# A local attention slot in a new order: GpSimd makes the low parts of the weights and the first squares

## What is computed

```python
for i in range(6):
    x = attn_layer(shift_tokens(x), Wqkv[i], q_scale[i], k_scale[i], Wo[i]) + x
    x = ffn_layer(shift_tokens(x), ln_g[i], ln_b[i], W1[i], b1[i], W2[i], b2[i]) + x

def attn_layer(x, Wqkv, qs, ksc, Wo):        # 16 heads of 64, x is (4, 256, 256)
    q, k, v = heads(split(x @ Wqkv))
    q, k = rotary(l2norm(q) * qs), rotary(l2norm(k) * ksc)
    ...                                      # windows of 64 that look one window back
    return softmax(q @ k.T * 8, masked) @ v @ Wo

def ffn_layer(x, g, bln, W1, b1, W2, b2):
    xn = (x - mu) / sqrt(var + 1e-5) * g + bln
    a, gate = split(xn @ W1 + b1)
    return a * gelu(gate) @ W2 + b2
```

## Time and profile before

| | |
|---|---|
| device time, median of 3 runs | 2144.07 us (2141.39 to 2149.77) |
| the profiled execution | 2145.24 us |
| its span | 2143.4 us |
| TensorE busy | 2040.7 us, 95% of the span |
| TensorE weight loads | 1704.1 us, 80% |
| DVE busy | 1723.7 us, 80% |
| ACT busy | 1392.7 us, 65% |
| GpSimd busy | 550.3 us, 26% |
| mean granted clock of TensorE | 0.99 |

### The profile page before, as it was taken

The page is one execution under the profiler, slowest core; times in us unless marked ns, Lnnn a source line. Parts: engine busy times, 40 slices in busy tenths (PEclk is TensorE's granted clock), DMA queues, the critical chain, the costliest instruction groups (busy, mean ns, idle before and its releaser), DMA issues.

```text
span 2143.4 us, 51804 instructions
## 1 busy us (share of the span) xinstructions
PE 2040.7 (95%) x17400; PEld 1704.1 (80%) x17400; DVE 1723.7 (80%) x4874; ACT 1392.7 (65%) x4026; POOL 550.3 (26%) x317
## 2 busy tenths in 40 slices
PE   5999999999998998999999999999999999999988
PEld 4787887887886676888888888888888888888877
DVE  6786787787676498898889888898889888988883
ACT  3776567567564355676767676866777676767653
POOL 2111111111111334232323233232323242323220
PEclk9999999999999999999999999999999999999999
DMA  3000000000000410021102011201120111011010
GB/s 120 8 10 1 7 12 1 7 12 1 6 26 0 140 31 15 13 72 33 56 14 72 14 58 31 72 14 46 44 73 14 34 57 52 25 33 55 14 33 20
DMA packets 50017, 72.10 MB, mean 34 GB/s; under 512 B 9429, under 2 KB 36869, under 8 KB 49541
## 3 DMA queue, kind: packets, MB, share of 16 engines
q1 hardware_dynamic: 47429, 64.30, 9.9%
q10 hardware_dynamic: 2368, 4.98, 0.6%
HBM read 51.58 MB, written 2.10 MB: 25 GB/s over the span
## 4 chain that ended last, share of the span: by engine, by line
PE 47%; issue 7%; DVE 4%; DMA 3%; ACT 3%; POOL 2%; SPq 1%; DVEq 0%; ACTq 0%; POOLq 0%
PE ps_loc L1722 17%; PE ps_loc L1830 7%; PE ps_loc L1799 5%; PE ps_loc L1761 4%; PE ps_loc L1841 4%; PE ps_loc L1772 4%; DMA late<-y_all 3%; PE ps_loc L1741 3%; PE ps_loc L1788 3%; POOL rnorm L2655 2%; PE ps_loc L1342 1%; ACT xnT_high L2077 1%; ACT pT L2060 1%; ACT xnT_loc L2077 1%; DVE w_low L2259 0%
## 5 line engine op out<-in xcount | busy, mean ns | idle before, releaser
L2655 POOL TENSOR_TENSOR rnorm<-norm_floor,half_loc 128x32 f32<-128x32 f32 x48 | 300.5, 6261 | 582.7 <-DVE norm_floor L2270 385.2
L1722 PE MATMUL ps_loc<-w_high,xT 128*128 128x512 f32 x1152 | 379.3, 410 | 0.7 <-ACT qk L2032 0.6
L2053 ACT ACTIVATE prob_loc<-prob_loc,top_loc 128x128 f32<-128x128 f32 x768 | 299.2, 402 | 45.2 <-DVE top_loc L2334 43.2
L718 ACT ACTIVATE prob<-prob,new_top 128x256 f32<-128x256 f32 x512 | 252.2, 497 | 0.0
L1722 PEld LDWEIGHTS ps_loc<-w_high,xT 128*128 128x128 f32 x1152 | 203.9, 189 | 51.4 <-issue 9.3
L2334 DVE CUSTOM_DVE_ANT_0 prob_loc<-ps_loc,const,rnorm 128x128 f32<-128x128 f32 x768 | 218.8, 345 | 28.0 <-PE ps_loc L1761 25.8
L1722 PE MATMUL ps_loc<-w_low,xT 128*128 128x512 f32 x576 | 228.5, 397 | 0.0
L2045 ACT ACTIVATE qT_loc<-ps_loc 128x512 f32<-128x512 f32 x96 | 57.4, 598 | 238.1 <-PE ps_loc L1741 238.1
L923 DVE CUSTOM_DVE_ANT_0 prob<-ps_cross,bias 128x256 f32<-128x256 f32 x512 | 184.7, 420 | 20.7 <-PE ps_cross L494 11.1
L1799 PE MATMUL ps_loc<-wo,qT_loc 128*128 128x256 f32 x768 | 169.8, 379 | 1.3 <-ACT qT_loc L2067 1.3
L1179 POOL TENSOR_TENSOR o<-o,alpha 128x1024 f32<-128x1024 f32 x32 | 61.0, 1906 | 425.1 <-DVE o L962 333.4
(11 more groups left out here) (214 smaller groups left out, 4869.0 us busy)
## 6 DMA issues: line engine op xcount, KB each, us to landing
w_raw<-in_ffn_Wqkv_dram SPq DMA_DIRECT2D x24, 512.0 KB, 5.7
w_raw<-in_ffn_Wqkv_dram SPq DMA_DIRECT2D x24, 256.0 KB, 3.9
wo<-in_ffn_Wo_dram SPq DMA_DIRECT2D x24, 256.0 KB, 3.5
v_mid<-v_even SPq DMA_DIRECT2D x24, 256.0 KB, 3.4
v_mid<-v_odd SPq DMA_DIRECT2D x24, 256.0 KB, 3.7
w<-in_ffn_W_dram SPq DMA_DIRECT2D x12, 341.0 KB, 3.3
w<-in_ffn_W_dram SPq DMA_DIRECT2D x6, 640.0 KB, 4.6
ctx_raw<-in_ctx_dram SPq DMA_DIRECT2D x12, 256.0 KB, 2.8
```

The source lines that it names most:

```text
L718: ins = act.activation(prob[:, t, h, :], prob[:, t, h, :], ACT.Exp, bias=new_top[:, t, h:h + 1], scale=-1.0, accum_out=chunk_sum[:, t, h:h ...
L1722: ins = pe.matmul(ps[:, DENSE + j % 2, :], xT[:, px, kk, t * P:(t + 1) * P], wqkv[pw][:, kk, col:col + 512], start=kk == 0 and n == 0, sto ...
L2053: ins = act.activation(pr, pr, ACT.Exp, bias=top[:, h, t:t + 1], scale=-1.0, accum_out=total[:, h, t:t + 1])
L2655: pool.tensor_tensor(rnorm[:, b % 2, t, :], norm2_floor[:, :], half[:, :], ALU.pow).then_inc(rnorm_done, 8)
```

## The change

Seven things, all in the local stage:

1. TensorE turns pair 4 ahead of `out(1)`, and xn ahead of the last projection. The turned xn goes to bank 4 and the turned x to bank 5 (both free of scores once pairs 0 to 5 are read), no longer to banks 0 and 1.
2. `pT` has three buffers instead of two.
3. ACT makes only the high part of the turned xn (`xn_high`); DVE makes the fp32 copy (`xn_copy`) with two tensor_scalar from PSUM, behind it `xn_low`.
4. ACT takes the first projection out ahead of the first exponentials, pairs 3 to 7 in other places among the copies, loads the table of the exponential with an exponential of one element (`exp_warm`), and makes all high parts of the next layer's weights at the end of slot 2.
5. DVE has another order: `minima(2)` and `share(0)` ahead of `moments`, `share(1)` ahead of `normal`, `minima(7)` behind `minima(6)`, cosines and sums of tile 0 behind `xn_low`, `norms(n, 1)` ahead of the last twists, with the `gated` units spread between.
6. GpSimd makes all 12 low parts of the next layer's weights, not DVE.
7. GpSimd makes the squares of tile 0 with a tensor_tensor of 128x2048, not ACT.

Cut to its core:

```diff
+    TURNED = 3
-        pT = sb("pT", [P, 2, 2, TT, P])
+        pT = sb("pT", [P, TURNED, 2, TT, P])
+        XN_TURN, X_TURN, FIRST_X = 4, 5, DENSE + 1
...
@@ TensorE, turn_x
-                pe.wait_ge(qkv_done, a)
+                    bank = X_TURN
+                    pe.wait_ge(s_read, now + 2 * RING)
@@ turn_qk
+                    if g == 1 and turned:
+                        pe.wait_ge(xT_done, a + 2 * U)
@@ widen
-                    pe.wait_ge(xnT_copied, a + U)
-                if m == 1 and turn:
-                    pe.wait_ge(xT_done, a + 4 * U)
+                    pe.wait_ge(xnT_high, a + U)
+                if m < 2:
+                    pe.wait_ge(u_done, a)
+                if m < 2 and ahead:
+                    pe.wait_ge(qkv_done, a + 2 * U + (SLOTS - 1 if m == 0 else U))
@@ slot
                 turn_probs(a, 3)
+                if ffn:
+                    turn_xn(f, a)
                 if ahead:
                     project(n, nb, 11)
-                if ffn:
-                    turn_xn(f, ahead)
+                turn_probs(a, 4)
                 out(a, L, b, 1)
-                turn_probs(a, 4)
                 if turn:
-                    turn_x(L + U * (b + 2), (b + 2) % B)
+                    turn_x(L + U * (b + 2), (b + 2) % B, a)
                 turn_probs(a, 5)
@@ ACT, probs_out
-                act.wait_ge(o_full, a + 4 * (pair // 2))
+                act.wait_ge(o_full, a + (4 * ((pair - TURNED) // 2 + 1) if pair >= TURNED else 0))
@@ slot, the order after it (a: attention, n: next, f: feed-forward)
+ q_out, exp_warm, qkv 0, exps 0, exps 1, qkv 1, qkv 2, exps 2, qkv 3, probs 0, qkv 4,
+ exps 3, probs 1, qkv 5, exps 4, qkv 6, exps 5, qkv 7, probs 2, qkv 8, exps 6, o_out 0,
+ qkv 9, exps 7, qkv 10, probs 3, xn_high, qkv 11, probs 4, x_out, probs 5, gates 0, gates 1,
+ squares(n, 1), probs 6, gates 2, probs 7, gates 3, o_out 3, gates 4, gates 5,
+ in slot 2: weights_high 0 to 11
@@ DVE
+            def xn_copy(a, L, b):
...
+                for kk in range(KD):
+                    ins = dve.tensor_scalar(xnT[:, kk, :], ps[:, XN_TURN, kk * T:(kk + 1) * T], vec[:, V_FG + kk:V_FG + kk + 1],
+                                            vec[:, V_FB + kk:V_FB + kk + 1], ALU.mult, ALU.add)
@@ slot, the order after it
+ k_out, minima 0, minima 1, minima 2, inverse 0, share 0, moments, inverse 1, share 1, normal,
+ inverse 2, minima 3, 4, 5, share 2, twists(0, 0), inverse 3, share 3, minima 6, 7, inverse 4,
+ share 4, norms(n, 0), inverse 5, share 5, twists(0, 1), inverse 6, share 6, xn_copy, xn_low,
+ cosines_both, o_out 1, gated 0, inverse 7, share 7, gated 1, o_out 2, sums(n, 0), gated 2,
+ x_low, gated 3, norms(n, 1), gated 4, twists(1, 0), scaled_keys 0, gated 5, twists(1, 1),
+ cosines k, sums, cosines q, q_sum, scaled_keys 1, add_attention, add_ffn
@@ GpSimd
+            def squares(a):
+
+                pool.wait_ge(qkv_done, a + 4)
+                pool.wait_ge(norm2_done, a)
+                pool.tensor_tensor(square, qk[:, 0, :], qk[:, 0, :], ALU.mult).then_inc(square_done, 8)
...
                 for b in range(1, B - 1):
                     norm(L + U * (b - 1), i, b - 1)
+                    squares(L + U * (b + 1))
                     rotate(L + U * (b + 1), b + 1)
                 if not last:
+                    for h in range(4):
+                        weights_low(L + LAYER, h)
                     pool.wait_ge(scale_in, loads(i * 32 + 64))
                     tables(L + LAYER, i + 1)
-                norm(L + U * (B - 2), i, B - 2)
+                    for h in range(4, 8):
+                        weights_low(L + LAYER, h)
+                root(L + U * (B - 2))
                 if not last:
+                    weights_low(L + LAYER, 8)
+                ffn_bias(L + U * (B - 2), i, B - 2)
+                if not last:
+                    squares(L + LAYER)
+                    for h in range(9, PIECES):
+                        weights_low(L + LAYER, h)
                     rotate(L + LAYER, 0)
```

More of the change, by code:

```diff
@@ L1556, in local_layers @@
         gate = sb("gate", [P, 2, T])
+        exp_warm = sb("exp_warm", [P, 1])
         qT = k.sb("qT_loc", [P, PAIRS, T], F32, ctx, "right")
@@ L1724, in project, with turn_qk @@
                 ins.then_inc(qkv_full, 1 if j < SLOTS - 1 else U - SLOTS + 1)
-            def turn_qk(a, first):
+            def turn_qk(a, first, turned):
                 pe.wait_ge(rope_done, a + U)
@@ L1874, in slot @@
                 n, nb = L + U * (b + 1), (b + 1) % B
-                turn_qk(a, b == 0 and not ffn)
+                turn_qk(a, b == 0 and not ffn, ahead)
                 scores(a, 0)
@@ L2074, in xn_out @@
                 act.wait_ge(xnT_full, a + U)
-                for dst in (xnT_parts[HIGH], xnT):
-                    for kk in range(KD):
-                        ins = act.activation(dst[:, kk, :], ps[:, DENSE, kk * T:(kk + 1) * T], ACT.Identity,
-                                             bias=vec[:, V_FB + kk:V_FB + kk + 1], scale=vec[:, V_FG + kk:V_FG + kk + 1])
-                ins.then_inc(xnT_copied, U)
+                for kk in range(KD):
+                    ins = act.activation(xnT_parts[HIGH][:, kk, :], ps[:, XN_TURN, kk * T:(kk + 1) * T], ACT.Identity,
+                                         bias=vec[:, V_FB + kk:V_FB + kk + 1], scale=vec[:, V_FG + kk:V_FG + kk + 1])
+                ins.then_inc(xnT_high, U)
             def widening_high(L, first):
@@ L2105, in slot @@
                 q_out(a)
-                exps(a, 0)
+                act.activation(exp_warm[:, :], zero[:, :], ACT.Exp)
                 if ahead:
                     qkv_out(n, nb, 0)
+                exps(a, 0)
                 exps(a, 1)
@@ L2117, in slot @@
                 if ahead:
-                    squares(n, 0)
                     qkv_out(n, nb, 4)
+                exps(a, 3)
                 probs_out(a, 1)
-                exps(a, 3)
                 if ahead:
                     qkv_out(n, nb, 5)
+                exps(a, 4)
+                if ahead:
                     qkv_out(n, nb, 6)
-                exps(a, 4)
                 exps(a, 5)
@@ L2128, in slot @@
                     qkv_out(n, nb, 7)
+                probs_out(a, 2)
+                if ahead:
                     qkv_out(n, nb, 8)
-                probs_out(a, 2)
                 exps(a, 6)
+                o_out(a, 0)
                 if ahead:
                     qkv_out(n, nb, 9)
-                o_out(a, 0)
+                exps(a, 7)
                 if ahead:
@@ L2177, in slot @@
                     gates(f, 5)
+                if split:
+                    for h in range(PIECES - 3):
+                        weights_high(L + LAYER, h)
                 if split:
@@ L2425, in _, with slot @@
              first_y) = linear_vector(dve)
-            def slot(L, b, i, shifts, ffn, ahead, turn, split=False, late=False, first=False):
+            def slot(L, b, i, shifts, ffn, ahead, turn, first=False):
                 a = L + U * b
@@ L2468, in slot @@
                 inverse(a, 3)
+                share(a, 3)
+                minima(a, b, 6)
+                minima(a, b, 7)
+                inverse(a, 4)
+                share(a, 4)
                 if ahead:
                     norms(n, 0)
+                inverse(a, 5)
+                share(a, 5)
+                if ahead:
                     twists(n, nL, 0, 1)
-                share(a, 3)
-                minima(a, b, 6)
+                inverse(a, 6)
+                share(a, 6)
+                if ffn:
+                    xn_copy(f, L if b else L - LAYER, fb)
+                    xn_low(f)
                 if ahead:
                     cosines_both(n, 0)
-                inverse(a, 4)
-                minima(a, b, 7)
-                share(a, 4)
-                inverse(a, 5)
-                inverse(a, 6)
-                if ahead:
-                    sums(n, 0)
-                share(a, 5)
-                if ffn:
-                    xn_low(f)
-                if split:
-                    weights_low(L + LAYER, 0)
-                if turn:
-                    x_low(L + U * (b + 2))
-                inverse(a, 7)
                 o_out(a, 1)
-                share(a, 6)
-                if split:
-                    weights_low(L + LAYER, 1)
                 if ffn:
                     gated(f, 0)
-                o_out(a, 2)
+                inverse(a, 7)
                 share(a, 7)
@@ L2500, in slot @@
                     gated(f, 1)
+                o_out(a, 2)
+                if ahead:
+                    sums(n, 0)
+                if ffn:
+                    gated(f, 2)
+                if turn:
+                    x_low(L + U * (b + 2))
+                if ffn:
+                    gated(f, 3)
+                if ahead:
+                    norms(n, 1)
+                if ffn:
+                    gated(f, 4)
                 if ahead:
@@ L2537, in layer @@
```

(6 more changed lines are left out.)

172 lines of the change are left out of this document (69 added, 103 removed).

## The result

The changed kernel takes 2156.99 us (median of 7 runs, 2155.24 to 2162.10) against 2144.84 us before in the same comparison (7 runs): ratio 1.0059, 95% interval 1.0046 to 1.0072. It is slower, by 12.2 us, where 6 us less were forecast; the time lies 1 us above the range on record. The profiled execution took 2159.01 us with a span of 2157.2 us.

A forecast was written before the change was run, and what follows sets the result against it. TensorE was taken as the bound of the middle 22 slots. The terms -15.3 -1 -10.5 +20.9 +6 -3 -1 gave -3.9 us, slot lengths -7; -6 was taken: 2139 us profiled, 2138 beside the median, range 2117 to 2156.

The forecast's parts named there:

- cost 2: Low parts on GpSimd behind slot 2's second power: slot 3 projections wait, 1.2 us a layer, 6 us in five.
- Gain 1: Pair 5's wait for ACT's pT copy ends: 15.3 us in 21 slots, plus 1 us for layer 5's slot 2.
- gain 2: Waits of slots 1 to 3 for share(0) and pT copies go: 2.5 us a layer, 10.5 us in all.
- VectorE's account: VectorE sheds 8 us of low parts in slots 2 and 3, takes xn_copy, 1.1 us a slot: no cost.
- Cost 1: GpSimd's squares, 4.6 us, hold share(2), so TensorE waits 0.95 us at pair 2: 20.9 us in 22 slots.
- rival A: Squares hardly hold VectorE: 0 to 8 us of cost, time 2117 to 2126 us, chance 0.26.
- Ends: Shorter key wait behind the first slot with its clock saves 3 us, the last slot 1 us, the tail 0.
- Rival B: Low parts come too late in slot 3, losing turns to VectorE: 35 us, time 2149 to 2167, chance 0.22.
- Clock: Behind the first slot: transposes save up to 2.4 us if the granted clock stays up, within a joint 3 us.

The follow-up runs named there:

- e1: Changed kernel with GpSimd's low parts of layers 1 to 5 replaced by a two-column product and a zero fill: 2127.86 us, ratio 0.9915.
- e15: e6 with out(1) ahead of turn_probs(4) again and both pairs of xn copies on ScalarE, none on VectorE: 2132.00 us.
- e6: e5 with the squares of the first tile back on ScalarE: 2123.38 us, ratio 0.9890.
- e7: Kernel before with only a third pT buffer, TensorE's order as it was: 2142.17 us, ratio 0.9991.
- e9: e7 with turn_probs(4) moved ahead of out(1): 2145.51 us, ratio 0.9996.
- e2: Changed kernel with GpSimd's squares cut to 64 of 2048 columns: 2154.24 us, ratio 1.0035.
- e4: Changed kernel with one more wait: GpSimd makes W1's low parts in slot 0 only behind VectorE's last scaled keys: 2150.21 us.
- e3: Changed kernel with one more wait: GpSimd starts the next layer's low parts only behind VectorE's last scaled keys of slot 2: 2146.29 us.
- e13: e6 with out(1) put ahead of turn_probs(4) again: 2133.14 us, ratio 0.9944.
- e5: Changed kernel with the waits of e3 and e4 and a new order of GpSimd's work in slot 3: 2123.39 us, ratio 0.9898.
- e10: e5 with low parts 0 to 3 made earlier, by GpSimd between slot 2's two powers, their high parts by ScalarE mid-slot: 2139.51 us.
- e8: Kernel before with only the twelve low parts of layers 1 to 5 moved from VectorE to GpSimd: 2148.39 us, ratio 1.0016.

## Why the prediction was wrong

The step that failed is cost 2. It let the low parts queue behind the second power of slot 2 and walked them through with VectorE's runs between them, so it counted what VectorE does to the pieces (6 us), and never what the pieces do to VectorE's last four runs, on which `turn_qk` waits. The rows for it were there: scaled keys of 2.59 us in place of 1.22 beside a weight subtraction. The four runs took 0.88 to 1.06 us more each, 4.06 us together. The slack is what e1 shows, keys done at 1385.26 and `turn_qk` at 1386.38, 1.1 us. That leaves 2.9 us, and TensorE waited 2.84 us behind four of the five slots 2 and 3.17 behind the first, before any clock and before slot 3. e1 measured the term at 29.1 us of medians instead of 6. What I did price was off too: pieces 6 and 7 were ready 6.7 us into slot 3, not 11.3, and only `project(9)` waited, 0.55 us.

Point by point:

- *Gain 1*: the wait went, but the agreement in size is luck. The pT waits of TensorE fell by 16.8 us against 16.3 forecast, yet that holds slot 2's waits too, which gain 2 had; the wait of gain 1 was 0.63 us a slot (0.73 in the forecast), 13 us in 21 slots. TensorE's order and the second pair of xn copies, which the forecast names as its cause, are worth 8.6 us (e15 against e6). e7 and e9 show that in the kernel before the buffer and TensorE's order gave none of it.
- *Gain 2*: right in slots 1 and 2, not shown in slot 3. In e6 slots 1 and 2 of layer 2 are 0.01 and 0.24 us above slot 0, where 0.53 and 0.92 stood before; slot 3 is still 1.05 above it (1.06 before), with the pieces in it. In e1, without them, slots 3 are 0.4 us above the later slots 1 on average.
- *VectorE's account*: `xn_copy` took 539 ns an instruction against 0.54 us forecast and cost nothing. That the power ends before VectorE asks was true as well, yet it is what let GpSimd's pieces loose with four of VectorE's runs still to come (4.9 us of them in e1). The power's 5.45 us in place of 6.3 added to that.
- *Cost 1*: mechanism right, size wrong. 3605 ns instead of 4.6 us, below my lower bound of 3.8: the bounds were taken from products with two different inputs, and this one reads the same rows twice (that this is the reason was not tested). So 20.9 us became about nothing in slots 0 to 2, as rival A had it; in slot 3 e2 puts it at 1.6 us a layer, and the whole at 2.8 us of medians.
- *Ends*: the wait went the wrong way. Behind the first slot it grew from 4.04 to 6.7 us, since W1's low parts held the same runs; the first two slots together still came out 0.9 us shorter, where 3 were forecast, and the last slot 0.5 us longer instead of 1 shorter. e4 gave 2.7 us back in the first slot and 1.4 to 1.7 us in each later slot 0, which I had at 55.6 by another count.
- *Rival B* has the time (2149 to 2167) but not the mechanism: the loss did not come from low parts that VectorE's runs had starved, as the earlier trace rows had suggested (they were held too, 1.97 for 1.3 us, but `project(9)` waited only 0.55); it came from VectorE, which lost a turn to every piece. That the time fell there is luck.
- *Clock*: no term for it beyond the first slot. In three slots 3 the half clock cost 2.7, 2.8 and 1.6 us, from the first transpose to the first score.

With both costs at nothing, the forecast's own sum is 2145.2 - 15.3 - 1 - 10.5 - 3 - 1 = 2114 us; e6's profiled execution took 2120.0 us. Most of the gains were there, though not all where they were forecast, and the loss came from one missing line: what each piece takes from VectorE.

The Trainium skill ("SBUF — State Buffer", Who interferes with whom) says that a VectorE instruction with two SBUF inputs contends with a GpSimd one that reads SBUF, and not with one that only writes it. The trace agrees on both: 2.28 us beside the low parts, 1.22 us beside e1's fills. It also says that who issues first blocks the other. Here, with both queues full, that comes out as strict turns.

## What to carry to other kernels

Work moved to GpSimd is not free because GpSimd is idle: for each product, ask which VectorE runs with two SBUF inputs lie beside it, charge each one up to a whole instruction of hold, and follow the last of them to who waits. Where that sum exceeds the slack, a semaphore can hold GpSimd back behind VectorE's deadline. Alone it gave 10.7 us here (e3), since the pieces then held what stood behind; with W1's wait and a new order it gave 33.6. And test a wait's cure in both directions: added to the kernel before, the buffer and TensorE's order did nothing (e9), while taking TensorE's order back from e6 cost 9.8 us (e13).

## What the runs showed of the hardware

- Four GpSimd products of 128x512 and four VectorE products of 128x1024, both queued back to back, alternated one for one, each VectorE run 0.9 to 1.05 us longer. But a turn can be lost: `share(0)` took 2.79 us in e3 with two pieces beside it. GpSimd is held as well: a two-column product took 0.19 us in e1 where nothing held it and 0.7 to 1.0 us beside VectorE's runs.
- A GpSimd fill of 510 columns took 0.52 us and held no VectorE run.
- A GpSimd product of 2048 columns with one tensor as both inputs took 3.6 us in the changed kernel, also where a `share` was held beside it, 4.05 us in slot 3 of e5 and 4.58 us in e10.
- Behind waits of TensorE of 2.8 to 3.2 us at one place, the transposes ran in whole or in part at the 1.2 GHz level in 3 of 5 cases in the changed kernel and in 4 of 5 in e2 and in e4, so the length of the wait alone does not decide it.
- GpSimd's power lasts 5.45 us in the changed kernel and in e6, and 6.26 us before and in e7, e8 and e9; the bias addition 1.28 against 1.58 us. Neither the squares, nor the low parts, nor the third buffer, nor TensorE's order makes the difference. What does stays open.
